# Keys in token order, read by the score products with a stride of four elements

## The reference

```python
# block 0: 16 heads of 64, relative bias, softmax over 128 keys, then an MLP of 1024
qh, kh, vh = (einsum('btd,hed->bhte', ln(v), W) for v, W in ((x, Wq), (ctx, Wk), (ctx, Wv)))
p = softmax((einsum('bhte,bhse->bhts', qh, kh) + rel_bias[idx]) / 8)
x = x + (p @ vh) @ fc_w.T + fc_b
x = x + gelu(ln(x) @ W1.T + b1) @ W2.T + b2
# block 1: 16 query heads of 16, ONE key and value head of 16, window of +-64 tokens
q, k, v = x @ Wq + bq, ctx @ Wk + bk, ctx @ Wv + bv
p = softmax(where(window, q @ k.T / 4, -1e9))
attn = (p @ v) @ Wo + bo
gate = silu([attn, x] @ Wg + bg)
out = attn * gate + x * (1 - gate)
x_hat = rms_norm(out) * rms_w
return x_hat - mean(x_hat, over tokens)
```

## Time and profile before

| | |
|---|---|
| device time, median of 3 runs | 1903.36 us (1902.6 to 1907.44) |
| profiled execution, first to last instruction | 1903.7 us |
| instructions | 55010 |
| PE busy | 1840.5 us, 97% |
| PEld busy | 1696.0 us, 89% |
| DVE busy | 1518.9 us, 80% |
| ACT busy | 1538.4 us, 81% |
| POOL busy | 1294.2 us, 68% |

### The profile page before, as it was taken

How to read it: one execution, slowest core, us unless ns; L and a number is a source line. 1 busy time by engine, 2 the same in 40 slices (tenths; PEclk the granted TensorE clock), 3 DMA queues, 4 the chain that set the end, 5 groups by cost and what they waited for, 6 DMA issues and landing times.

```text
span 1903.7 us, 55010 instructions
## 1 busy us (share of the span) xinstructions
PE 1840.5 (97%) x18660; PEld 1696.0 (89%) x18660; DVE 1518.9 (80%) x6787; ACT 1538.4 (81%) x5586; POOL 1294.2 (68%) x1328
## 2 busy tenths in 40 slices
PE   5999999999999999999999999999999999999974
PEld 4899999999999999999999999999999999999963
DVE  6768888888888888888888888888888888878764
ACT  4688888888888888888888888888888888888864
POOL 3547776767776767777766777766777776777654
PEclk9999999999999999999999999999999999999997
DMA  6434444444444444454434454444444444444332
GB/s 208 131 84 116 111 119 111 115 110 115 107 118 120 115 107 114 104 123 121 116 99 121 101 125 118 114 102 118 111 118 118 110 107 113 112 116 114 88 83 56
DMA packets 215273, 214.49 MB, mean 113 GB/s; under 512 B 29904, under 2 KB 197456, under 8 KB 214992
## 3 DMA queue, kind: packets, MB, share of 16 engines
q1 hardware_dynamic: 214992, 210.97, 44.5%
HBM read 67.23 MB, written 9.44 MB: 40 GB/s over the span
## 4 chain that ended last, share of the span: by engine, by line
PE 94%; DMA 2%; DVE 1%; ACT 1%; POOL 1%; issue 1%; SPq 0%; ACTq 0%; DVEq 0%; POOLq 0%
PE bank L576 12%; PE bank L577 11%; PE bank L578 11%; PE bank L594 8%; PE bank L590 8%; PE bank L591 8%; PE bank L757 7%; PE bank L770 7%; PE bank L582 4%; PE bank L882 4%; PE bank L895 3%; PE bank L583 3%; PE bank L586 3%; PE bank L654 2%; PE bank L600 2%
## 5 line engine op out<-in xcount | busy, mean ns | idle before, releaser
L2574 ACT ACTIVATE soft<-soft,row_min 128x128 f32<-128x128 f32 x1024 | 397.4, 393 | 16.3 <-DVE row_min L1728 16.0
L2494 ACT ACTIVATE soft<-soft,row_min 128x128 f32<-128x128 f32 x1024 | 397.8, 394 | 9.5 <-DVE row_min L1620 9.1
L235 DVE STREAM_TRANSPOSE turned<-soft 128x512 f32<-128x512 f32 x512 | 349.2, 692 | 9.7 <-POOL soft L3032 4.9
L3032 POOL TENSOR_TENSOR soft<-soft,inv_sum 128x512 f32<-128x512 f32 x256 | 267.1, 1044 | 127.3 <-DVE inv_sum L1628 123.3
L3041 POOL TENSOR_TENSOR soft<-soft,inv_sum 128x512 f32<-128x512 f32 x256 | 264.9, 1045 | 93.0 <-DVE inv_sum L1737 93.0
L1620 DVE CUSTOM_DVE_ANT_0 soft<-bank,relb 128x128 f32<-128x128 f32 x1024 | 231.6, 284 | 64.9 <-PE bank L757 64.5
L1728 DVE CUSTOM_DVE_ANT_0 soft<-bank,winb 128x128 f32<-128x128 f32 x1024 | 226.6, 284 | 16.9 <-PE bank L882 14.5
L2494 ACT ACTIVATION_READ_ACCUMULATOR soft<-soft,row_min 128x1 f32 x1024 | 196.7, 192 | 0.0
L2574 ACT ACTIVATION_READ_ACCUMULATOR soft<-soft,row_min 128x1 f32 x1024 | 195.1, 191 | 0.0
L1691 DVE TENSOR_TENSOR hidS<-hid,hidS 128x1024 fp32r<-128x1024 f32 x64 | 120.5, 1883 | 71.5 <-ACT hidS L2545 68.6
L757 PE MATMUL bank<-kT,qT 64*128 64x128 f32 x2048 | 148.7, 285 | 1.5 <-DVE kT L1600 1.4
(11 more groups left out here) (255 smaller groups left out, 6538.3 us busy)
## 6 DMA issues: line engine op xcount, KB each, us to landing
soft<-turned SPq DMA_DIRECT2D x1024, 128.0 KB, 2.8
tokens<-stats_by_row SPq DMA_DIRECT2D x63, 256.0 KB, 3.3
tokens<-in_x SPq DMA_DIRECT2D x32, 256.0 KB, 3.1
raw<-in_x_t SPq DMA_DIRECT2D x32, 256.0 KB, 2.8
x<-in_x SPq DMA_DIRECT2D x32, 256.0 KB, 3.1
out<-gate SPq DMA_DIRECT2D x63, 128.0 KB, 3.1
tokens<-in_ctx SPq DMA_DIRECT2D x31, 256.0 KB, 2.8
raw<-in_ctx_t SPq DMA_DIRECT2D x31, 256.0 KB, 2.8
```

The costliest lines, as they stand in the source:

```text
L235: return eng.transpose(turned[:, slot, :, s % 2, :, :].rearrange("p j h b -> p h j b"), soft[:, s, :, :].rearrange("p h (j a) -> p h j a", ...
L2494: last = act.activation(soft[:, s, h, :], soft[:, s, h, :], ACT.Exp, bias=row_min[:, s, h:h + 1], scale=-1.0, accum_out=row_sum[:, s, h:h ...
L2574: last = act.activation(soft[:, s, h, :], soft[:, s, h, :], ACT.Exp, bias=row_min[:, s, h:h + 1], scale=-1.0, accum_out=row_sum[:, s, h:h ...
L3032: pool.tensor_tensor(soft[:, m % NS0, :, :], soft[:, m % NS0, :, :], inv_sum[:, m % NS0, :].unsqueeze(2).broadcast_to([P, QUAD, SEQ]), ALU ...
```

## The change

The copies `k_out` and `kv_turn` no longer permute: they read the bank in order and write `kT` and `kpar` in token order. The score products read the moving operand in the block order instead: for each j, the 32 elements 4a + j, so with a step of four float32 elements, 16 bytes. What arrives in the banks is the same as before, in the same columns, and all that follows is untouched. No instruction, wait, buffer or DMA is added, removed or moved.

```diff
@@ scores
                         last = pe.matmul(bank[i][:, h * SEQ:(h + 1) * SEQ], qT[half, c, b * SEQ:(b + 1) * SEQ],
-                                         kT[half, c, b * SEQ:(b + 1) * SEQ], start=True, stop=True)
+                                         kT[half, c, b * SEQ:(b + 1) * SEQ].rearrange("p (a j) -> p j a", j=NB),
+                                         start=True, stop=True)
@@ scores1
                         last = pe.matmul(bank[j][:, c * 2 * SEQ:(c + 1) * 2 * SEQ], q1T[tile, c, tok],
-                                         kpar[tile, :, tok], start=True, stop=True)
+                                         kpar[tile, :, tok].rearrange("p i (a j) -> p i j a", j=NB),
+                                         start=True, stop=True)
@@ kv_turn
                 for i in range(2):
-                    dve.tensor_scalar(kpar[:, i, :].rearrange("p (b j a) -> p b j a", b=GROUP, j=NB),
-                                      bank[:, 0:TOK].rearrange("p (b a j) -> p b j a", b=GROUP, j=NB), bk1[:, 0:1],
-                                      parity[:, i:i + 1], ALU.add, ALU.mult)
+                    dve.tensor_scalar(kpar[:, i, :], bank[:, 0:TOK], bk1[:, 0:1], parity[:, i:i + 1], ALU.add, ALU.mult)
@@ k_out
                 for c in range(QC):
                     i = Q * QC + c
-                    last = dve.tensor_scalar(kT[:, c, :].rearrange("p (b j a) -> p b j a", b=GROUP, j=NB),
-                                             bank[:, c * TOK:(c + 1) * TOK].rearrange("p (b a j) -> p b j a", b=GROUP, j=NB),
-                                             bk[:, i:i + 1], None, ALU.add)
+                    last = dve.tensor_scalar(kT[:, c, :], bank[:, c * TOK:(c + 1) * TOK], bk[:, i:i + 1], None, ALU.add)
```

## The result

| | before | after |
|---|---|---|
| device time, median | 1904.56 us (4 runs) | 2072.73 us (2071.66 to 2072.98, 4 runs) |
| profiled execution | 1903.7 us | 2071.1 us |
| DVE busy | 1518.9 us | 1496.6 us |

What follows compares the result with a forecast made beforehand. PE's own work was taken to bound the loop. Profiled span 1903.7 - 0.4 (head) + 0 (strided read) = 1903.3 us, the median 0.4 below, so 1902.9 us; range for 8 in 10: 1899 to 2070 us.

Steps and rivals of the forecast that it cites:

- What bounds the kernel: In the loop PE waits only 0.6 us together, so time added to a PE instruction counts in full, DVE savings nothing.
- The copies: DVE's copies L1600 and L1572 get simpler, 19 us less DVE work hidden under PE; -0.4 us, bounds 0 and -1.4.
- The term of 60 ns for each copy: Each of DVE's 256 + 64 copies at L1600 and L1572 gets 60 ns shorter by reading PSUM in order.
- The 0.4 us of the head: In the head, PE's three waits for `kT` shrink, two shorter copies before each product: 0.4 us may come back.
- The strided read: PE's score products L757 and L882 read their moving operand with a 16-byte step; claimed free, + 0 us, chance 0.56.
- the lower end: For L757 and L882 on PE, the 16-byte step costs nothing: 0 us.
- The two outer bounds: For the step in L757 and L882: no cost at least, a stream taking twice as long, 164 us, at most.
- The half-speed rival: Score products L757 and L882 hold their partitions twice as long, 214 or 428 ns: +164 us, 2067 us; chance 0.26.
- The partial slowdown: Score products slow to L1600's strided pace, 1.34 ns an element, or less: +98 us, 2001 us, anything from 1910; chance 0.14.
- The marks that I gave for reading the result: Signs in the profile: L757 at 272 ns if free, near 336 if partly slowed, 379 with batches near 2 us if halved.

## Why the prediction was wrong

**What bounds the kernel** was right. PE was hardly ever kept waiting in the loop (3.5 us idle of 1550 before, 3.4 us of 1700 after), so every nanosecond added to a product counted: 173 us of longer batches gave 168 us.

**The copies** were wrong in size, without effect. The term of 60 ns for each copy (bounds 0 to 81) is 0 to 1 ns. I had compared a tensor-scalar copy with tensor-tensor sums and put the difference on the step, having named the other reading, that it belongs to the form of the operation; it was that one. The 0.4 us of the head did not come either: L757 waits 1.4 us for `kT` as before. DVE's busy time did fall, by 22 us where I had said 19, and this is a trap, for the copies have no part in it. It is one line elsewhere, L1691 before and L1689 after:

```profile
L1691 DVE TENSOR_TENSOR hidS<-hid,hidS 128x1024 fp32r<-128x1024 f32 x64 | 120.5, 1883 | 71.5 <-ACT hidS L2545 68.6
```

```profile
L1689 DVE TENSOR_TENSOR hidS<-hid,hidS 128x1024 fp32r<-128x1024 f32 x64 | 98.8, 1544 | 74.1 <-ACT hidS L2543 69.8
```

With the copies alone changed DVE stays at 1517.5 us; with block 0's products alone slow it is at 1495.0. Yet slow products do not save DVE's time as such: with the step of eight and with the step on the stationary operand L757's batches are as long, and L1691 takes 1994 and 1979 ns on average, more than before. What differs is how the second L1691 of a turn meets one operation on POOL. The changed kernel, then the step of eight (start, us):

```profile
546.08 1.19 DVE L1689 TENSOR_TENSOR hidS<-hid,hidS 128x1024 fp32r<-128x1024 f32 x1
546.08 2.34 POOL L3109 TENSOR_TENSOR x<-x,rows 128x512 f32<-128x512 f32 x1
```

```profile
535.91 2.32 DVE L1691 TENSOR_TENSOR hidS<-hid,hidS 128x1024 fp32r<-128x1024 f32 x1
535.85 1.30 POOL L3111 TENSOR_TENSOR x<-x,rows 128x512 f32<-128x512 f32 x1
```

Starting together, DVE takes 1.19 us and POOL 2.34; when POOL starts 0.06 us ahead, POOL takes 1.30 us and DVE 2.32. This repeats in 26 places of each of the two runs, with POOL 0.01 us ahead to 0.04 behind in the one and 0.04 to 0.07 ahead in the other. Before, the same DVE instruction started at 504.17 us, while POOL was in the operation ahead of this one (503.81 to 505.12), and took 2.03 us. So the saving hangs on which of two engines comes first, by less than 0.1 us, and 26 x (2.03 - 1.19) = 22 us is about all of it. It is luck, and worth nothing in the loop.

**The strided read** is the step that failed: "I take the lower end. The nearest row is L1600." It put + 0 us into the sum for a term that measured 173 us in the batches. The two outer bounds came from PE's own rows, and the upper one, 164 us, was short by only 9, but the choice between them rested on a row of another engine and another memory. L1600 reads PSUM on DVE; the products read SBUF on PE. Moreover its 1.34 ns an element was not the price of the step at all: in order, the same copy takes 474 ns too. The comparison that I leaned on was also worked out wrongly. From 1.03 to 0.84 ns PE's pace is 23% more, not a third, and against the 1.34 ns of the strided row it is 60% more. A row that near to the contiguous pace seemed to speak for a free read, and said nothing of SBUF. The one piece that did speak of it, the rule of the Trainium skill that an engine needs two hits on a 16-byte line ("Advanced Engine Details and Errata", section "SBUF Cachelines"), I set aside at 0.26. The float32 runs agree with it closely: 0.84 ns an element with four hits on a line, 0.86 with two, 1.72 with one. The fp32r runs do not: with two hits on a line, step of two or pairs, the pace is halved, 0.90 ns in place of 0.46. The sentence of the Trainium skill in "SBUF — State Buffer", section "Door 1: The DMA port swizzle", that four float32 are a free step is refuted by 1.72 ns. I should have noticed that the two sentences do not have equal weight: one says how the memory works, and by that mechanism a step of exactly one line cannot be free.

**The half-speed rival** is what happened, at 2067 us forecast and 2072.7 measured. It was mis-sized by term: 107 ns more for each step became about 113, since the pace went to a little over double (1.72 against 0.84 ns); the 164 us was 115 + 58 = 173, less 6 us that came back in head and tail. That small excess put the result just above the range, whose upper end of 2070 left nothing for it. **The partial slowdown** at DVE's pace had no basis, as that pace was none. A slowdown of that kind exists, though, at a step of three.

The marks that I gave for reading the result were enough to tell the cases apart at once: L757 at 402 (379 named for half speed), L883 at 625 (588), batches at 2.06 us, DVE's waits for L757 longer by 0.8 us a time (175.6 us in 126 against 64.5 in 109), other PE lines unchanged, no new waits of PE in the loop.

## What to carry to other kernels

Where a permutation has to be made somewhere, make it where VectorE copies out of PSUM: there a step of four float32 cost nothing (475 against 474 ns). On TensorE's operands count the 16-byte lines for each element: in float32 up to half a line was free to within 0.03 us a batch, three quarters and more were not; for fp32r even a step of two halved the pace. When the only priced rows for an unseen pattern come from another engine or another memory, they bound nothing: give the mechanism that would forbid the pattern the weight of a coin at least, and put some slack beyond its price in the range.

## What the runs showed of the hardware

- A float32 product takes its moving operand at 0.84 ns an element or about 1.73 ns a 16-byte line of SBUF, whichever is longer (seven patterns, table above; the step of eight came to 1.77). A boundary matters, not only the distance: aligned pairs 1.19 us a batch, the same pairs moved by three elements 2.08 us.
- The stationary operand pays too: 326 against 188 ns for 128 columns with a step of 16 bytes.
- fp32r at 0.46 ns an element keeps its pace only on the contiguous operand; steps of two and four and aligned pairs of neighbours all came to 0.90 ns.
- Two element-wise operations on two SBUF tiles that start almost together, one on DVE (1024 columns) and one on POOL (512), did not both run at full pace. Within 0.04 us of each other DVE took 1.19 us and POOL 2.34; with POOL ahead by 0.06 us POOL took 1.30 and DVE 2.32.
- DVE out of PSUM, 256 float32 in the tensor-scalar form: no difference between a step of 4 and a step of 16 bytes, and none for writing with a step of two (475 ns in the run with interleaved sequences).
